# A latent attention's projections made inside the steps of the state space layer before it, and kept in DRAM; one PSUM bank instead of two for that layer's C rows

## What is computed

```python
# layer 0, a state space layer run in both directions (d = forward, backward)
xz = layernorm(x) @ W_in.T;  u = silu(conv4(xz_u));  z = xz_z            # 512 channels
dt, B, C = split(u @ Wx_d.T, [64, 16, 16])
delta = softplus(dt @ Wdt_d.T + bdt_d)
h[t] = exp(delta*A)*h[t-1] + delta*B*u;   y = sum over 16 states of h*C  + u*D
x = x + (y_forward + y_backward)*silu(z)/2 @ W_out.T
# layer 1, the latent attention: 8 samples, 16 heads of 64
lat = layernorm(layernorm(x))*g_l + b_l      # 256 rows a sample
med = layernorm(context)*g_m + b_m           # 77 rows a sample
q = lat @ Wq;  k, v = split(concat(lat, med) @ Wkv)     # 333 keys
x = x + softmax(q k^T / 8) v @ Wout
```

## Time and profile before

| | us |
|---|---|
| median of 3 runs | 4219.45 |
| profiled execution, first to last instruction | 4219.3 |
| layer 0, first scan to last product | 71 to 1020 |
| last X of layer 0 written | 1030.9 |
| layer 1, first row maximum | 1065.6 |
| last X of layer 1 written | 1581.9 |

### The profile page before, as it was taken

One profiled execution on the slowest core, in us unless ns is written; L12 is line 12 of the kernel. 1 busy time (PEld: TensorE's weight loads), 2 busy tenths in 40 slices (PEclk: granted clock), 3 DMA queues, 4 the chain that ended last, 5 costly groups with the idle time before them and its releaser, 6 DMA issues. The chain is left out here.

```text
span 4219.3 us, 57578 instructions
## 1 busy us (share of the span) xinstructions
PE 3754.1 (89%) x20106; PEld 2591.3 (61%) x20106; DVE 3071.9 (73%) x7148; ACT 2286.6 (54%) x5527; POOL 1378.4 (33%) x937
## 2 busy tenths in 40 slices
PE   5777878777999998999999999888899889889998
PEld 2323333223666667998788887555566558645777
DVE  6989899897666667666787886677577784554777
ACT  5676767754644442222455556757677652343446
POOL 3989899995000000000233223366321100010000
PEclk8989989898999999999999999889999999988999
DMA  3444434344000000000000001000000000100000
GB/s 117 142 132 146 148 125 156 130 152 146 1 1 1 1 1 33 21 31 1 14 1 1 1 1 42 2 14 1 12 2 2 19 23 1 42 1 20 1 1 21
DMA packets 83283, 180.17 MB, mean 43 GB/s; under 512 B 9035, under 2 KB 14259, under 8 KB 80307
## 3 DMA queue, kind: packets, MB, share of 16 engines
q1 hardware_dynamic: 82995, 176.49, 12.5%
HBM read 173.84 MB, written 2.62 MB: 42 GB/s over the span
## 5 line engine op out<-in xcount | busy, mean ns | idle before, releaser
L209 PE MATMUL PS<-db,cst 128*128 128x512 f32 x1024 | 537.2, 671 | 159.7 <-DVE db L1260 159.7
L1255 DVE TENSOR_TENSOR_SCAN db<-PS,db 128x512 f32<-128x512 f32 x512 | 590.7, 1204 | 36.7 <-ACT PS L1220 27.9
L209 PEld LDWEIGHTS PS<-db,cst 128*128 128x128 f32 x1024 | 205.2, 211 | 466.9 <-DVE db L1260 244.6
L216 PE MATMUL PS<-cst,p 128*128 128x128 f32 (+1 forms) x2880 | 393.3, 282 | 48.1 <-DVE pt L3295 16.7
L216 PEld LDWEIGHTS PS<-cst,p 128*128 128x128 f32 (+1 forms) x2880 | 332.9, 147 | 106.7 <-issue 35.9
L209 PE MATMUL PS<-xnT,W 128*128 128x256 f32 (+2 forms) x1072 | 330.7, 455 | 19.4 <-ACT pt L2826 7.9
L1201 POOL TENSOR_TENSOR db<-W,b 128x1024 f32<-128x1024 f32 x128 | 312.5, 2470 | 1.9 <-PE PS L209 1.8
L1201 POOL TENSOR_TENSOR db<-du,b 128x1024 f32<-128x1024 f32 x128 | 307.9, 2432 | 6.6 <-PE PS L209 5.8
L209 PEld LDWEIGHTS PS<-xnT,W 128*128 128x128 f32 (+1 forms) x1072 | 210.2, 200 | 137.9 <-issue 89.0
L2035 POOL TENSOR_TENSOR rb<-rb,tb 128x512 f32<-128x512 f32 x32 | 42.9, 1342 | 758.2 <-DVE tb L2030 758.2
L1693 ACT ACTIVATE p<-PS,sm 128x333 f32<-128x333 f32 x320 | 168.7, 538 | 164.8 <-DVE sm L1686 161.9
(11 more groups left out here) (469 smaller groups left out, 8512.2 us busy)
## 6 DMA issues: line engine op xcount, KB each, us to landing
b<-bc_rows SPq DMA_DIRECT2D x256, 256.0 KB, 3.4
c<-bc_rows SPq DMA_DIRECT2D x256, 256.0 KB, 3.5
W<-in_we SPq DMA_DIRECT2D x9, 1024.0 KB, 4.8
W<-in_w SPq DMA_DIRECT2D x1, 4224.0 KB, 12.3
W<-in_w SPq DMA_DIRECT2D x1, 4122.5 KB, 14.0
W<-in_w SPq DMA_DIRECT2D x1, 4100.0 KB, 12.3
W<-in_w SPq DMA_DIRECT2D x1, 2313.0 KB, 8.3
X<-in_x SPq DMA_DIRECT2D x4, 512.0 KB, 14.5
```

The lines of the kernel that those rows point to most:

```text
L209: ins = T.matmul(out, l, r, start=first and i == 0, stop=last and i == len(pairs) - 1)
L216: ins = T.transpose(bank[0:m, c:c + r], s, ident[0:r, 0:r])
L1255: V.tensor_tensor_scan(db[:, f, r], self.ring.PS[:, self.BANKS[x % 3], r], db[:, f, r], 0.0, ALU.mult, ALU.add).then_inc(self.sc.sem, 1)
```

## The change

1. A new class `Fore`. In 100 of the steps of layer 0 that have no piece of PE, PE makes one bank of layer 1's projections, ACT copies it out one step later, and SP stores it in DRAM six steps after it was made. Made are: the context's keys (16 outputs of 308 columns) and values (12 outputs) and q, k and v of chunks 0 to 2, that is samples 0 to 5 (72 outputs of 512 columns). SP loads their weights in blocks to four buffers.
2. `Latent` loads q, k and v from there: q and k with one DMA for each unit, and v with one or two for each sample. It still projects samples 6 and 7 itself. The gain and bias on the context move to ACT in layer 0. POOL's copies go.
3. The norm of chunks 0, 1 and 2 is made in layer 0, from steps 83, 147 and 211 on; the norm of chunk 3 stays in layer 1.
4. C has one PSUM bank. ACT copies C after both exponentials, once the product before it is done. The ring has 4 banks.
5. SP loads the weights of layers 1 and 2 behind the loads of the first eight units.

The diff, cut to its core:

```diff
-    CBANKS = (3, 4)
+    CBANKS = (4,)
...
-        self.nxt.early = {0: 171, 1: 235}
-        self.nxt.late, self.nxt.dense = {2: -1, 3: 4}, True
+        self.nxt.early = {0: 83, 1: 147, 2: 211}
+        self.nxt.late, self.nxt.dense = {3: -1}, True
+        self.fore = Fore(E, mine[:, offsets(SPEC[0])[1]:WREG], self.todo)
...
     def sp(self, e):
-        self.steps(e, self.nothing, self.nothing, self.sp_piece, self.sp_b, self.sp_c, self.nothing)
-        for token in (self.aa(2 * self.NU), self.gb(self.NU), self.du_(8), self.cv(14), self.dt(8), self.diag(1)):
-            e.wait_ge(*token)
-        self.E.load_next(e, self.n)
+        self.steps(e, self.nothing, self.nothing, self.sp_piece, self.sp_b, self.sp_c, self.nothing, self.fore.sp)
...
             for x in self.todo[i]:
                 piece(e, *x)
+            fore(e, i, self.nxt)
...
-            if f == 0 and not self.on_pool(i):
-                self.act_c(e, i)
+        if not self.on_pool(i):
+            self.act_c(e, i)
...
-        e.wait_ge(*self.h(i - self.pools(i) - 1))
+        e.wait_ge(*self.h(i - self.pools(i)))
...
+class Fore:
+    CHUNKS, START, LATEST = 3, (27, 102, 166, 230), 6
...
+        self.blocks = [("kc", 0, f) for f in range(0, 8, 2)] + [("vc", 0, j) for j in range(4)]
+        for c in range(self.CHUNKS):
+            self.blocks += [("qk", c, f) for f in range(8)] + [("v", c, j) for j in range(4)]
+        free = [i for i in range(len(todo)) if i >= 224 or not any(
+            x[0] in (Mamba.GATE, Mamba.OUT) or x[0] == Mamba.READY and x[2] in Mamba.ON_PE for x in todo[i])]
...
+        for i, s in enumerate(self.START):
+            k = self.early if i == 0 else 24
+            self.steps += [x for x in free if x >= s][:k]
...
+    def sp(self, e, step, norm):
...
+        if step in self.store_at:
+            self.sp_store(e, self.store_at[step])
+        for n in self.load_at.get(step, ()):
+            self.sp_weights(e, n)
...
+    def pe(self, e, step, norm):
+        if step not in self.steps:
+            return
...
+        e.wait_ge(*self.win[self.slot[n]](self.nth[n]))
...
+        bank = self.ring.take(e, ("fore", o), self.kept(o + 1))
...
+        elif kind == "qk":
+            ins = mm(T, bank, [(split(w[:, 256 * x:256 * x + 256], 2)[:, k, :],
+                                self.E.xnT[:, k, c * 512:(c + 1) * 512]) for k in range(2)])
...
+    def act(self, e, step, norm):
...
+        if step - 1 not in self.steps:
+            return
...
+        e.wait_ge(*self.made(o + 1))
+        e.wait_ge(*self.sent[o % 2](o // 2))
+        C.activation(self.st[o % 2][0:rows, 0:cols], self.ring.of(("fore", o))[0:rows, 0:cols], ACT.Copy,
+                     scale=0.125 if kind == "qk" and x == 0 else 1.0).then_inc(self.kept.sem, 1)
...
 class Latent(Layer):
...
+    def sp_heads(self, e, u):
+
+        b, f = divmod(u, 8)
+        at = 0 if b < self.begun else 2 * S
+        e.wait_ge(*self.pe_s(4 * (u - 7)))
+        e.eng.dma_start(self.qk[:, f, at:], self.fore.qkd[b, f, :, at:]).then_inc(self.qkl[f].sem, 16)
...
+    def sp_all(self, e):
+
+        for token in self.fore.stored():
+            e.wait_ge(*token)
+        for u in range(self.NU):
+            self.sp_heads(e, u)
+            if u == 1:
+                self.sp_values(e, 0)
+            elif u == 7:
+                self.E.load_weights(e, self.n)
+                self.sp_values(e, 1)
+                self.E.load_next(e, self.n)
+            elif u >= 18 and u % 8 == 2:
+                self.sp_values(e, u // 8)
...
         if self.many:
-            out = [(0, i) for i in range(14)] if u == 0 else []
-            if f >= 3:
-                out.append((b + 1, f - 3))
-            elif f == 0 and b > 0:
-                out.append((b, 5))
+            out = [(b + 1, f - 3)] if 3 <= f < 3 + self.vp else []
             if f >= 2:
                 out.append((b + 1, self.vp + f - 2))
-            elif b > 0:
+            else:
                 out.append((b, self.vp + f + 6))
-            return [x for x in out if x[0] < NB]
+            return [x for x in out if self.begun <= x[0] < NB]
```

More of the change, by code:

```diff
@@ L921, in sp_c, with steps @@
         e.eng.dma_start(self.c_[i % 4], self.bc[k, 16 + s].partition_broadcast(P)).then_inc(self.cd_[i % 4].sem, 16)
-    def steps(self, e, norm, nxt, piece, one, two, three):
+    def steps(self, e, norm, nxt, piece, one, two, three, fore):
         for j in self.FIRST:
@@ L982, in pool @@
         self.enter(e)
-        self.steps(e, self.nothing, self.nothing, self.pool_piece, self.pool_b, self.nothing, self.pool_c)
+        self.steps(e, self.nothing, self.nothing, self.pool_piece, self.pool_b, self.nothing, self.pool_c, self.nothing)
     def pe_piece(self, e, what, k, j):
@@ L1337, in setup @@
         self.cw = min(512, inner)
[L1338 to L1341, removed]
+        self.begun = 2 * Fore.CHUNKS if self.many else 0
+        self.vp = (2 if self.many else 3) * inner // self.cw
+        nv = (NB - self.begun) * self.vp
+        self.pv = E.counted("pe_v", nv)
+        na = [(nv + 1) // 2, nv // 2]
         self.va, self.vd = E.counted("act_v", na[0]), E.counted("dve_v", na[1])
         if self.many:
[L1344 to L1349, removed]
-        else:
+            m = 8 * (NB - self.begun)
+            self.pq, self.qa, self.pk, self.kd = [E.counted(x, m) for x in ("pe_q", "act_q", "pe_k", "dve_k")]
+            self.fore = self.prev.fore
+            self.qkl = [E.counted(x, NB, 16) for x in ("sp_b0", "sp_b1", "sp_b2", "sp_c0", "sp_c1", "sp_c2", "sp_x0",
+                                                       "sp_x1")]
+            self.vl = [E.counted(x, NB // 2 + self.begun // 2, 16) for x in ("sp_x2", "sp_x3")]
+        else:
+            self.cg = split(E.tile(f"cg{n}", 1232), 2)
+            self.cgt = E.counted("dve_cg", 1)
             self.setup_bias("bo", 1)
@@ L1417, in pool @@
         self.enter(e)
-        if self.many:
-            self.pool_pairs(e)
-        else:
+        if not self.many:
             self.pool_batches(e)
@@ L1502, in dve @@
         self.enter(e)
[L1503 to L1510, removed]
-        if not self.many:
+        V, W = e.eng, self.W
+        if not self.many:
+            e.wait_ge(*self.w_ready)
+            for tok in self.E.ctx_ready:
+                e.wait_ge(*tok)
+            for k in range(2):
+                ins = V.tensor_scalar(self.cg[:, k, :], self.E.cnT[:, k, :], W["xg"][:, k:k + 1], W["xb"][:, k:k + 1],
+                                      ALU.mult, ALU.add)
+            ins.then_inc(self.cgt.sem, 1)
             self.dve_bias(e)
@@ L1546, in pe_piece @@
         e.wait_ge(*self.w_ready)
-        e.wait_ge(*self.cgt(1))
+        if not self.many:
+            e.wait_ge(*self.cgt(1))
         if i < self.vp:
@@ L1721, in pe_values @@
         b, f = divmod(u, self.F)
-        for i in range(self.vp):
-            e.wait_ge(*self.v_ready(b, i))
+        for token in self.v_tokens(b):
+            e.wait_ge(*token)
         e.wait_ge(*self.ptd(u + 1))
```

188 lines of the change are left out of this document (152 added, 36 removed).

## The result

The changed kernel takes 4141.8 us in the median of 4 runs (4136.1 to 4150.6); the kernel before, run beside it, 4219.5 us (4 runs, 4218.5 to 4225.4). The ratio is 0.9818, with a 95% interval of 0.9804 to 0.9831: 78 us faster, where 117 were forecast. The profiled execution is the slowest of the four, 4150.6 us with a span of 4148.8, so that the differences between stretches of the two profiles add up to 70.5 us and not to 78.

What follows compares the result with a forecast made beforehand. The prediction took PE to bound layer 1, and in layer 0 saw DVE and POOL busiest. From 4219.3 us, -160 in layer 1 and +43 in layer 0 gave 4102 us, range 4055 to 4165.

Steps and rivals of the forecast that it cites:

- bubbles: Layer 1: DVE, next in line, no longer hides norms beneath PE; 10 us, bounds 0 and 40.
- Rival B: Layer 1: DVE or the round trip bounds it, bare units 5.0 instead of 4.23 us; +35, 4137 us; chance 0.11.
- the sum of layer 0: Layer 0: PE 4, gate 7, softplus 18, third norm 8, other norms 6; +43 us, range 6 to 110.
- the part on SP and DMA: Layer 0: about 150 more DMAs sharing SP's queue with loads of B and C cost nothing, bounds 0 and 15.
- lost lead: Layer 0, C bank: ACT starts its pieces later; where pieces are longer, up to 2.3 us of lead lost.
- The gate's 7: Layer 0: ACT's gate piece of 5.1 us exceeds the time that fits; 4 times +1.75, +7 us.
- The third chunk's norm: Layer 0: a third chunk's norm, two DVE passes and the loss by ACT; +8 us, bounds 6 and 12.
- PE was put at 4: Layer 0, steps 230 to 253: PE's sum and output exceed DVE's step; +4 us, bounds 0 and 7.
- rival C: Layer 0 hides nearly all as POOL and DVE waits overlap: +10, bubbles 5; 4064 us; chance 0.10.
- A: Layer 0: PE becomes the bound if its clock stays at 0.90; layer 0 +90, 4149 us; chance 0.12.
- D: Layer 0: SP's store waits for ACT's copy, delaying loads of B and C; +2.8 us a step, 4382; chance 0.05.
- The check named for "wrong": Layer 0, quiet steps: ACT idle at its new wait for DVE's product would show the forecast wrong; costed at nothing.

Runs made afterwards that it cites:

- the kernel without it: Changed kernel with its stores reading an area never rewritten, so ACT's copies wait for no store; stored contents wrong: 4081.1 us.
- 3 steps: Changed kernel with each store issued three of SP's steps after its output instead of six: 4076.1 us, and 4070.1 us when run again.
- that run: Changed kernel with stores reading a never rewritten area, and ACT's copies also cut to 8 columns: 4075.7 us.
- the first experiment: Kernel before, with only the single C bank of the change and ACT's later copy of C: 4232.7 us against 4219.3.
- the last version: Changed kernel with stores three steps after their outputs and the norm's L428 made by four products with a pointer to one column: 4066.2 us.

## Why the prediction was right in part

**Right: layer 1.** Forecast 391, measured 388.3. The start was 5 us and is 4.5 (1123.59 to 1128.07). Units, drain and bubbles were 357.6 + 18.7 + 10 = 386.3 and are 383.8. PE is busy for 357.5 of 365 us, at 0.99, so that DVE, next in line, did not take over. The bare units take 4.23 us, as forecast. In the waits from 1123 to 1512 us PE waits for none of the weights, costed at nothing.

One term of this sum was luck. The 10 us for bubbles were to come from DVE. Of the 383.8, 383.8 - 357.6 - 18.7 = 7.5 are left for them, and 5.2 of these are one wait of PE for a load of q and k; for DVE it waits 0.5 in all. From PE's timeline of the changed kernel, and from its DMA issues from 1120 to 1180 us:

```profile
1136.12 2.59 PE L209 MATMUL PS<-qk 64*128 64x333 f32 x8 [5.24 <-DMA qk<-fore_qk]
```

```profile
qk<-fore_qk SPq DMA_DIRECT2D x20, 294.5 KB, 10.4
```

In these 60 us such a load takes 10.4 us to land, not the 3.0 of the page's median. Ahead of the late one in SP's order stands a load of 1 MB of v, behind it the weights (4100 KB, issued at 1130.12). Which of them delayed it no run separates, so that the weights cost nothing isn't shown. The two waits for q and k, 8.8 us together, come again in other profiles, with 6.4 to 8.3 us in six of them. Rival B (4137) comes within 5 us of the measured time and is wrong, since its 35 us would stand in layer 1. A time that fits does not bear out a mechanism.

**Right: no slowdown, and something to pay in layer 0.** 4141.8 lies in the range of 4055 to 4165. Of the signs named, those of layer 1 came: bare units of 4.23 us and the first maximum after 4.5. Those of layer 0 did not: it ends 92.7 us later and not 35 to 55, DVE's idle time at the exponentials rose from 27.9 to 114.2, fourfold where it was to double, and PE's clock there is 0.92 and not 0.95 or more.

**Wrong: the sum of layer 0, +43 where +92.7 was measured.** The step that failed is the part on SP and DMA, "Nothing, bounds 0 and 15". It asked whether the new stores delay the loads of B and C. It did not ask who waits for a store. ACT does, at the copy after next, and that wait (two staging buffers, store six of SP's steps late, 4.5 to 5.4 us from issue to landing in the three stores read above) had no term. It costs 71 us by the kernel without it, 76 to 81 by the two profiles with 3 steps. The forecast's range took it in only because its upper end allowed 110 us for layer 0, for copies and lost lead. Had the wait been costed, the bounds would have come from the same rows: a store behind a load of C that waits for a buffer, some 3.5 us of landing, against two steps of 3.13. The Trainium skill (DMA: Bandwidth & Descriptors, Latency and other measured facts) says that the receipt round trip to the target memory dominates a transfer's fixed cost, and that HBM is the slowest target. The runs agree as far as those three stores to DRAM take 4.5 to 5.4 us, and the loads of B and C, 256 KB each, 3.7 to 3.8; no run separates the receipt from the traffic beside it.

**The small terms.** The gate's 7 is the best of the forecast: its four steps cost 7.4 with the C bank alone, and quiet steps nothing, as said. The lost lead as a whole (gate 7, norms 6, and 6 to 8 of the 18 for softplus, by the first expectation) was put at about 20 and is 10.5. The third chunk's norm was put at 8; one norm costs about 5 where it now stands, but the sum left out what the two others give back where they stood, and the balance is 0.3. Moved norms and the single C bank together weren't tried without `Fore`. PE was put at 4, with a bound of 7; taking away half of its products gives 4.3. The copies on the path were worth 10 us by the expectation of that run and some 8 by the run. Without the store's wait layer 0 grows by 14 to 23 us (958.8 to 968.0 against 944.9), a third to a half of the 43: the forecast's own terms were 20 to 29 us too high, which cancelled about a third of the missing one. With that wait gone the kernel takes 4070 to 4081, between the forecast and rival C. That 4141.8 is only 40 us from 4102 is in this part luck.

**The rivals.** A (PE the bound, clock at 0.90, 4149) is near in time and near in its sign: the clock did stay at 0.92, and PE waits with POOL behind it. But PE waits for ACT's copy, 82 us in the waits; with the wait gone the clock is 0.98 in the dense stretch, and halving PE's added work changes little. There the low clock was an effect. D (SP blocks) named the right queue and the wrong direction: not the store holds up the loads, the loads hold up the store, and the six steps of distance, counted there as a protection, are the cause. (By the forecast's own sum D would outweigh the gain from 117 / 100 = 1.2 us a step on, not 1.6.)

**The check named for "wrong"** (ACT idle at its wait for DVE's product) came, 100 us of it, and meant little, as the first experiment shows. Idle time of an engine with slack is no sign.

## What to carry to other kernels

When work is added that stores its results, cost the buffer's whole round trip: from the copy, past everything that stands ahead of the store in its queue, to the landing, and back to the copy that reuses the buffer. With two buffers that must fit in two steps. Place a store in the queue as soon as its data can be there: behind loads that wait for the layer's own progress it closes a loop, and each step can then take the whole way round it. Don't put it too early either: with 3 steps the queue already waits 230 us for the data, with loads behind it. Three or more staging buffers may serve too; that wasn't tried, nor were two C banks together with `Fore`.

## What was not expected of the hardware

With the store after 4 steps, one tiny instruction of the norm took 10.29 us, and another just before it, on the same 4 columns, 0.15. Timeline of DVE in that kernel:

```profile
396.07 0.15 DVE L426 RECIPROCAL stat<-stat 128x4 f32<-128x4 f32 x1
396.25 10.29 DVE L428 SCALAR_TENSOR_TENSOR stat<-stat 128x4 f32<-128x4 f32 x1
406.47 2.33 DVE L1255 TENSOR_TENSOR_SCAN db<-PS,db 128x512 f32<-128x512 f32 x2
```

The timeline of POOL over the same time:

```profile
390.32 7.02 POOL L1201 TENSOR_TENSOR db<-du,b 128x1024 f32<-128x1024 f32 x3
397.26 2.38 POOL L1240 TENSOR_TENSOR db<-db,c 128x1024 f32<-128x1024 f32 x1
399.58 6.96 POOL L1201 TENSOR_TENSOR db<-du,b 128x1024 f32<-128x1024 f32 x3
```

POOL works from 390.32 to 406.54 without a gap, and DVE's instruction ends when POOL stops. L428 reads two tensors from SBUF, L426 only one. The Trainium skill (SBUF — State Buffer, Who interferes with whom) says that a DVE instruction with two SBUF inputs contends with a GpSimd (POOL) instruction that reads SBUF, and that whichever comes second is blocked for the whole of the other. The trace agrees on the kind of instruction; here the block lasts over five POOL instructions in a row. With 5 steps the same 10.3 us appear once, with 6 and 3 they don't (1.2 us at most in layer 0): it seems to hang on how POOL's burst falls. That is why the last version replaced L428. Its timeline, against the same place with 3 steps:

```profile
254.53 0.58 DVE L429 TENSOR_SCALAR stat<-stat 128x1 f32<-128x1 f32 x4
...
393.52 0.58 DVE L429 TENSOR_SCALAR stat<-stat 128x1 f32<-128x1 f32 x4
```

```profile
255.50 1.14 DVE L428 SCALAR_TENSOR_TENSOR stat<-stat 128x4 f32<-128x4 f32 x1
```

Four instructions with the second factor given as a scalar of each partition took 0.58 us together in both places, and none of the 44 from 60 to 1130 us took over 0.21. The one they replace had 0.16 to 1.15 with 3 steps, and 10.29 where it fell badly. The time can't be told from that with 3 steps alone, which had no such stall to lose. That the new form also takes the 10 us away wasn't tried on a kernel that has them.
